# Second attention: transposes issued in pairs, a third half of scores in PSUM, and the stage written out instead of looped

## The reference

```
q = _fq_sym(q * scale);  k = _fq_sym(k);  v = _fq_sym(v, axis=keys)       # 16 heads of 32
attn = softmax(einsum('bhqd,bhkd->bhqk', q, k))                           # 1024 x 2048 a head
attn = clip(round(attn / s), 0, 255) * s,  s = max(attn over keys) / 255
out  = einsum('bhqk,bhkd->bhqd', attn, v)
```

## Time and profile before

| | us |
|---|---|
| median of three runs | 1657.66 |
| the profiled execution, its own time | 1657.65 |
| its span in the trace | 1655.9 |
| second attention, first matmul of scores to last product | 1125.8 to 1490.4 |
| TensorE busy over the span | 1417.4 |
| VectorE busy over the span | 1020.5 |

### The profile page before, as it was taken

The page is one execution under the profiler, slowest core; times in us unless marked ns, Lnnn a source line. Parts: engine busy times, 40 slices in busy tenths (PEclk is TensorE's granted clock), DMA queues, the critical chain, the costliest instruction groups (busy, mean ns, idle before and its releaser), DMA issues.

```text
span 1655.9 us, 23143 instructions
## 1 busy us (share of the span) xinstructions
PE 1417.4 (86%) x7965; PEld 683.2 (41%) x8012; DVE 1020.5 (62%) x1717; ACT 757.4 (46%) x1090; POOL 437.0 (26%) x324
## 2 busy tenths in 40 slices
PE   7993888888856999999999999667888888869778
PEld 3441555555544444444444444322323333324334
DVE  5998999999854011101111101677989999964995
ACT  4774888888810111111111111215777777762553
POOL 1114100000004768999910000311111111100341
PEclk9996999999958899999999999885555555559989
DMA  7997555564209999999987889369999999992001
GB/s 246 290 275 166 106 126 126 116 132 98 54 1 365 375 349 380 380 394 405 396 327 296 294 310 305 114 132 196 206 209 217 218 214 215 213 199 76 1 1 51
DMA packets 506455, 354.91 MB, mean 214 GB/s; under 512 B 419736, under 2 KB 421784, under 8 KB 505760
## 3 DMA queue, kind: packets, MB, share of 16 engines
q1 hardware_dynamic: 491744, 304.94, 68.4%
q0 software_dynamic: 10816, 40.90, 7.5%
q10 hardware_dynamic: 3840, 8.39, 1.3%
HBM read 206.06 MB, written 38.01 MB: 147 GB/s over the span
## 4 chain that ended last, share of the span: by engine, by line
PE 46%; DVE 23%; issue 13%; DMA 11%; ACT 4%; POOL 2%; DVEq 1%; POOLq 0%; ACTq 0%; SPq 0%
PE scores L974 17%; PE bank L992 9%; DVE arena L1757 8%; DMA arena<-arena 7%; PE bank L880 4%; PE bank L864 2%; DVE arena L1543 2%; DVE arena L1529 2%; PE bank L863 2%; ACT arena L1261 2%; PE bank L1166 1%; PE bank L984 1%; POOL xs_d L689 1%; POOL arena L750 1%; DMA qst_d<-arena 1%
## 5 line engine op out<-in xcount | busy, mean ns | idle before, releaser
L1757 DVE TENSOR_SCALAR_CACHE_REDUCE arena<-scores,arena 128x1024 f32<-128x1024 f32 x256 | 318.3, 1281 | 30.3 <-PE scores L1040 25.7
L974 PE MATMUL scores<-arena 128*128 128x512 f32 x736 | 321.4, 595 | 4.3 <-DMA arena<-in_L_ffn_w 4.3
L1332 ACT ACTIVATE arena<-arena 128x2048 int16<-128x2048 f32 x128 | 256.2, 2002 | 130.8 <-POOL arena L765 93.1
L1689 DVE TENSOR_TENSOR arena<-scores,arena 128x512 f32<-128x512 f32 x46 | 31.8, 692 | 449.7 <-PE scores L974 449.7
L1040 PE MATMUL scores<-arena 96*128 96x512 bf16 x512 | 261.0, 620 | 54.4 <-DVE arena L1757 30.4
L974 PEld LDWEIGHTS scores<-arena 128*128 128x128 f32 x736 | 140.4, 191 | 181.1 <-issue 181.1
L992 PE MATMUL bank<-arena 128*128 128x512 f32 x368 | 165.0, 601 | 3.4 <-issue 3.3
L1529 DVE TENSOR_REDUCE arena<-scores 128x1 f32<-128x640 f32 (+3 forms) x128 | 127.7, 1018 | 8.1 <-PE scores L841 7.7
L1261 ACT ACTIVATE arena<-bank 128x512 f32<-128x512 f32 (+3 forms) x256 | 116.8, 507 | 25.8 <-PE bank L864 25.8
L1543 DVE TENSOR_TENSOR arena<-arena 128x1024 f16<-128x1024 f32 (+2 forms) x128 | 126.2, 1026 | 3.5 <-issue 1.8
L1289 ACT ACTIVATE arena<-scores 128x512 f32<-128x512 f32 x46 | 27.5, 597 | 215.7 <-PE scores L974 215.7
(11 more groups left out here) (268 smaller groups left out, 2061.1 us busy)
## 6 DMA issues: line engine op xcount, KB each, us to landing
arena<-in_L_ffn_w SPq DMA_DIRECT2D x69, 2048.0 KB, 12.5
arena<-arena SPq DMA_DIRECT2D x32, 256.0 KB, 3.0
kst_d<-arena POOLq DMA_DIRECT2D x16, 384.0 KB, 6.5
tern_d<-arena POOLq DMA_DIRECT2D x12, 512.0 KB, 7.0
arena<-kst_d SPq DMA_DIRECT2D x16, 384.0 KB, 4.2
xs_d<-arena SPq DMA_DIRECT2D x23, 256.0 KB, 3.5
arena<-xs_d SPq DMA_DIRECT2D x22, 256.0 KB, 12.9
ys_d<-arena ACTq DMA_DIRECT2D x22, 256.0 KB, 7.0
```

The lines of the kernel that those rows point to most:

```text
L974: ins = pe.matmul(scores[:, m * 1024 + half * 512:m * 1024 + half * 512 + 512], xsT[a][:, c], wa[:, m, c, half * 512:half * 512 + 512], st ...
L1332: act.activation(p16[t % PBUF], ssb[i], ACT.Exp, bias=ebias[i], scale=-1.0, accum_out=rsum[a][:, t:t + 1]).then_inc(p_ready, 1)
L1757: dve.tensor_scalar(ssb[i][:, s:s + 1024], scores[:, s:s + 1024], nsq[:, bass.ds(h, 1), t], None, ALU.mult, ALU.min, accum_out=nmx[i][:, h ...
```

## The change

Transposes: one DMA transpose now turns two tiles, 32 blocks (`p16[i]` holds two tiles, likewise `pT[i]`). There are 3 pair buffers of `p16` (PAIRS_P) and 2 pair buffers of `pT` (PAIRS_T). SyncE waits for the exponentials of both tiles and for the products of the pair two before; ScalarE waits, at the first tile of a pair, for the landing of the pair three before.

Scores: `bank4` and `bank5`, which the stage did not use, become columns 2048 to 3071 of `scores`, and the halves m = 2n, 2n+1 go round three places (m mod 3). A half waits for the reading of the half three before.

Buffers: `ssb` has 3 buffers instead of 4 (SBUFS), since the second pair of `pT` lies where one of them was.

Order: TensorE issues the products of tiles n-7 and n-6 together after the scores of each odd n. VectorE still finishes head h-1 after reading tile 6. GpSimd's `stage_v` comes after the bias of tile 6 instead of tile 5. The loop over heads is gone: TensorE, ScalarE and VectorE have all 128 tiles written out.

```diff
-PBUF = 4
-LAG = 3
+PAIRS_P, PAIRS_T = 3, 2
-SBUFS = 4
+SBUFS = 3
-        scores = stack.enter_context(nc.psum_tensor("scores", [P, 4 * 512], F32))
+        scores = stack.enter_context(nc.psum_tensor("scores", [P, 6 * 512], F32))
+        bank4, bank5 = scores[:, 2048:2560], scores[:, 2560:3072]
-        p16 = [r.take(I16, B * SK) for r in (rq, rq, over_xn3, over_xn3)]
-        pT = [r.take(F16, NC, P) for r in (rq, rq, over_xn3, over_xn3)]
+        p16 = [r.take(I16, 2, B * SK) for r in (rq, over_xn3, over_xn3)]
+        pT = [rq.take(F16, 2, NC, P)]
-        ssb += [wq_sb.rearrange("p c n -> p (c n)"), over_q3.take(F32, B * SK)]
+        ssb.append(over_q3.take(F32, B * SK))
+        pT.append(Region(early.start).take(F16, 2, NC, P))
@@ SyncE
-            for n in range(H * NT):
-                i = n % PBUF
-                if n >= PBUF:
-                    sp.wait_ge(av_done, n - PBUF + 1)
-                sp.wait_ge(p_ready, n + 1)
-                sp.dma_start_transpose(pT[i], p16[i].bitcast(F16)).then_inc(pT_in[i], 16)
+            for j in range(H * NT // 2):
+                i = j % PAIRS_T
+                if j >= PAIRS_T:
+                    sp.wait_ge(av_done, 2 * (j - PAIRS_T + 1))
+                sp.wait_ge(p_ready, 2 * j + 2)
+                sp.dma_start_transpose(pT[i].rearrange("p o c n -> p (o c) n"),
+                                       p16[j % PAIRS_P].rearrange("p o n -> p (o n)").bitcast(F16)).then_inc(pT_in[i], 16)
@@ TensorE
+            def a1_scores(n):
...
+                for m in (2 * n, 2 * n + 1):
+                    if m >= 3:
+                        pe.wait_ge(s_read, m - 2)
...
+            for n in range(H * NT):
+                a1_scores(n)
+                if n % 2 and n >= 7:
+                    a1_pv(n - 7)
+                    a1_pv(n - 6)
@@ ScalarE
+            def exp_tile(n):
...
+                if n % 2 == 0 and j >= PAIRS_P:
+                    act.wait_ge(pT_in[(j - PAIRS_P) % PAIRS_T], 16 * ((j - PAIRS_P) // PAIRS_T + 1))
...
-            sweep(act, H, a1_head)
+            for n in range(H * NT):
+                exp_tile(n)
@@ VectorE
-            sweep(dve, H, a1_head)
+            for n in range(H * NT):
+                read_scores(n)
+                h, t = divmod(n, NT)
+                if t == NT - 2 and h:
+                    finish_head(h - 1, (h - 1) % 2)
+            finish_head(H - 1, (H - 1) % 2)
```

## The result

The changed kernel takes 1663.78 us (median of six runs, 1662.43 to 1667.07), the kernel before on the same chip 1657.53 us: a ratio of 1.0043, 95% interval 1.003 to 1.0056, so 5.0 to 9.3 us slower. The forecast was 11.8 us slower: the direction is right and the size too large. The profiled execution is the slowest of the six, 1667.07 us, with a span of 1665.3 us, and so 9.4 us longer than the one profiled before. It reached the stage's first read 1.24 us later, at 1128.17; what follows is therefore counted from the first read.

A forecast was written before the change was run, and what follows sets the result against it. The prediction took SyncE's stream of DMA transposes, 22.18 us a head, as the bound of layer 1's second attention. Its terms 11.9 - 3 + 2.4 + 0.5 = +11.8 on 1657.65 gave 1669.5 us; own range 1663 to 1677, wider range 1645 to 1682.

The forecast's parts named there:

- Item 1: Loop written out: ten heads that fetched no instructions each take 1.19 us more, +11.9 us; bounds 0 to +18.
- Item 2: One transpose for two tiles: half the dips in the data rate at tile ends go away, -3 us.
- The upper bound: Most that writing the loop out could cost: whole halts of 1.5 us, one per 6.5 of 80 tiles, +18 us.
- items 3 and 4: Stage's start: first transpose waits for a second exponential, +2.4 us; its end: two products after the last landing, +0.5 us.
- the rival in which fetches cost nothing: Instruction-fetch halts are made up at 290 GB/s in the transpose stream: -0.1 us, 1657.5 us; chance 0.15.
- Item 5: Third half of scores and products in pairs on TensorE: cost 0; may remove some waits for scores.
- Item 6: Buffer rings and new waits: cost 0; pT ring 4.1 us a pair under the stream's 4.9, 0.8 us room.
- The starved ring: Rival: pairs land 9.4 us after issue, so the two-deep pT ring limits the stream, 27.5 more, 1697 us; chance 0.10.
- the fast rate for long transposes: Rival: paired transposes run at 290 GB/s, so VectorE's 21.4 us a head decides: -13.4 us, 1644.2 us; chance 0.18.

The follow-up runs named there:

- E4: Kernel before, but from tile 4 on only the first 8 of a tile's 16 blocks are transposed: 1640.6 against 1655.56 us, ratio 0.9904.
- E1: Kernel before with TensorE's, ScalarE's and VectorE's programs written out for all 16 heads, single transposes: 1669.39 against 1655.56 us, ratio 1.0078.
- E9: Kernel before with looped pairs, 4 ssb buffers, two halves, one product of a pair issued between score halves: 1657.93 against 1656.84 us, ratio 1.0005.
- E6: Kernel before with TensorE's program alone written out: 1666.06 against 1657.67 us, ratio 1.0051.
- E5: The changed kernel run once more, unedited, against the kernel before: 1665.12 against 1657.67 us, ratio 1.0048.
- E2: Changed kernel with two halves of scores instead of three, timed against the kernel before: 1667.37 against 1655.56 us, ratio 1.0069.
- E7: Kernel before with pairs in the loop, 4 ssb buffers, two halves, both products issued together: 1662.92 against 1657.67 us, ratio 1.0038.
- E10: Kernel before with loads of keys and queries of heads 2 to 15 cut to 16 x 2 elements: 1644.94 against 1656.84 us, ratio 0.9927.
- E8: Kernel before with key and query loads of heads 2 to 15 issued on GpSimd's queue instead of SyncE's: 1664.0 against 1657.67 us, ratio 1.0048.

## Why the prediction was right, and where it was off

*The whole.* The forecast had the mechanism, fetches that halt a stream of transposes, and the direction; 1663.78 lies at the low edge of its own range of 1663 to 1677, and its 11.8 us outside the measured 5.0 to 9.3. Nearly all of the difference is in items 1 and 2.

*What bounds.* Right: SyncE's queue is unbroken before and after, halving the bytes gains 15 us (E4), and the limit behind is 21.54 us a head, predicted as 21.4.

*Item 1, written out, +11.9.* By itself +12.9 us (9.8 to 16.1) in E1. Inside the change, with pairs, the ten heads lost 7.97 us, 0.80 a head instead of 1.19. This is the term that was mis-sized, since I took the price of a fetch from single transposes and used it for pairs. The upper bound took a halt as 1.5 us; rows 8 have 13 slices, 1.3 us, which lowers it from 18 to 16.

*Item 2, pairs, -3.* The reason was wrong, and so was the place. In looped code a pair saves nothing (E9). Where code is fetched it seems to: E1's and E6's 23.5 and 23.2 us a head became 22.97 and 22.90 in the changed kernel and E5, and 22.96 in E2, which has pairs but no third half. Heads 1 to 3 went from 23.37 to 22.70 us, but with pairs and two halves they took 23.04 (E2) and 23.14 (E9), so not all of these 2.02 us is the pairs' doing. This rests on one trace a run; the times do not tell E6 (1.0051) from the changed kernel (1.0043), which pays for items 3 and 4 besides. With 22.2 us for a head without fetches and 13 packets in ten heads, a fetch costs about 0.8 to 1.0 us with single transposes and 0.55 to 0.6 with pairs. The traces show where the difference lies. Counted from the DMA packets in slices of 0.1 us over heads 4 to 13:

| | fetches | under 20 GB/s, us | above 270 GB/s, us |
|---|---|---|---|
| single, looped (before) | 0 | 2.4 | 28 |
| single, written out (E1) | 13 | 20.3 | 49 |
| single, TensorE written out (E6) | 12 | 17 | 44 |
| pairs, looped (E9) | 0 | 3.5 | 24 |
| pairs, written out (changed kernel) | 13 | 20 | 57 |

The halts are alike, 1.2 to 1.4 us a fetch, and the burst that catches up lasts 1.3 to 1.6 us a fetch with single transposes and 2.5 with pairs. That it lasts longer because more is issued ahead when the halt ends is likely and was not tried by itself. Items 1 and 2 together: forecast +8.9, measured 7.97 - 2.02 - 0.92 = +5.0. The same holds for the rival in which fetches cost nothing: its mechanism is real, and it worked in part.

*Items 3 and 4, +2.4 and +0.5.* +2.35 for the first transpose. Behind the last landing the products end after 1.08 us instead of 0.65, +0.43. A pair lands at the soonest 6.7 us after issue, where 6.8 was worked out.

*Item 5, third half at no cost.* The time fits, the argument had a gap. I asked what the third half gains and not what the products in pairs cost: 0.4 to 0.7 us of VectorE's time a pair with two halves (E7), which E9 takes back in another way. In the changed kernel and in E2 the heads in the middle are equally long, 22.9 to 23.0 us, so there the slower stream hides it.

*Item 6, rings.* The outcome is right and the room was smaller than worked out: in the stream a pair lands 7.6 us after issue in the median, not 6.8, which makes (7.6 + 1.3) / 2 = 4.5 us a pair under 4.9, and products that come late use it up (E7). The queue is unbroken in the changed kernel and E9. The starved ring did not come, nor did the fast rate for long transposes: 216 GB/s.

*The loads.* "2.5 us a head are the loads" was right as a sum, but 1.2 of it is their issue and 1.3 their bytes (E10).

The Trainium skill's rule that crossing a 16 KiB block of instructions is mostly hidden ("Runtime: NRT & Kernel Launch", "Instruction fetch mechanics") does not hold for a kernel bound by a stream of DMA transposes: 13 us in E1. The Trainium skill's rule to merge many small transfers ("DMA: Bandwidth & Descriptors", "Rules for kernel authors") names transfers under 64 KB as mostly overhead. It does not reach these, which carry 0.5 MB each, and merging two of them brought nothing in E9.

## What to carry to other kernels

Lay each resource's own work of one loop pass end to end, the issuing queue of the DMA included; the idle times named here pointed at TensorE and VectorE, and the bound was the transposes. Where the DMA engines are the bound, a loop that has gone round once is worth keeping, since new instructions come through the same engines. When work is issued in larger pieces, ask what the piece holds up on its engine, and how many buffers cover it.

## What the runs showed of the hardware

The granted clock of TensorE in 1245.9 to 1445.8 was 0.50 before and 0.65 in the changed kernel (0.66 in E5), though its work is the same; it was 0.55 with two halves (E2), and 0.51 with looped pairs and two halves (E9):
```profile
1245.90:1445.80 199.90, 160.84 (x1400) 53.31 (x1398) 184.37 (x307) 145.71 (x140) 29.04 (x81) 0.55 1.14 211
```
```profile
1245.90:1445.80 199.90, 168.51 (x1442) 58.85 (x1442) 189.76 (x318) 151.08 (x146) 30.19 (x85) 0.51 1.12 215
```
These are E2 and E9. The clock alternates between its two levels, 1.2 and 2.4 GHz, where before it stayed at the lower one throughout the stage. What differs beside it is TensorE's waiting: its products stood idle for landings 82.5 us in the changed kernel (up to 4.6 at once) and 84.3 in E5, against 24.3 before, 20.7 in E9 and 18.2 in E2. Why E2's clock is still above that of before is open. The higher clock gained no time, since TensorE is not the bound. Plain loads from another engine's queue are no way round a stream of transposes: in E8 they cost at least as much as in SyncE's own, 22.57 us a head against 22.18.
